# GroupNorm attention over 1024 rows: the low part of v moved from VectorE to GpSimd, with a new order of both engines' work

## The reference

```
def reference(x, W_qkv, b_qkv):
    g = x.reshape(16, 64, 256, 32, 4)                  # 32 groups of 4 channels
    m, s = mean and variance of g over (rows, tokens, the 4 channels)
    n = ((g - m) / sqrt(s + 1e-5)).reshape(x.shape)
    qkv = einsum('bglc,dc->bgld', n, W_qkv) + b_qkv    # d = 384: q, k, v x 2 heads x 64
    score = softmax(einsum('bghlc,bghmc->bghlm', q, k) / sqrt(128))   # inside each row
    out = einsum('bghlm,bghmc->bghlc', score, v)       # back to (16, 64, 256, 128)
    return x + out
```

## Time and profile before

| what | value |
| --- | --- |
| median of 3 runs | 4220.36 us (4219.55 to 4224.01) |
| the profiled execution | 4225.53 us, span 4223.5 us |
| granted TensorE clock | 0.992 of full speed |
| busy: PE, DVE | 3958.7 us (94%), 3759.4 us (89%) |
| busy: ACT, POOL | 3125.2 us (74%), 2134.7 us (51%) |
| HBM | 134.42 MB read, 134.22 MB written |
| mean busy share of the 16 DMA engines | 0.7 to 0.9 in nearly all slices |

### The profile page before, as it was taken

The page is one execution under the profiler, slowest core; times in us unless marked ns, Lnnn a source line. Parts: engine busy times, 40 slices in busy tenths (PEclk is TensorE's granted clock), DMA queues, the critical chain, the costliest instruction groups (busy, mean ns, idle before and its releaser), DMA issues.

```text
span 4223.5 us, 147348 instructions
## 1 busy us (share of the span) xinstructions
PE 3958.7 (94%) x44133; PEld 2923.8 (69%) x44133; DVE 3759.4 (89%) x7138; ACT 3125.2 (74%) x8193; POOL 2134.7 (51%) x3089
## 2 busy tenths in 40 slices
PE   4999999899999999999999899999999999999998
PEld 3767777677776777767777677776767777677776
DVE  6998989889898898988989889898898989989887
ACT  3777777677776777767777677776777777777776
POOL 1555555455554555545555455554555555555554
PEclk9999999999999999999999999999999999999999
DMA  7999898998998989989899998989989998997878
GB/s 197 198 193 201 196 198 196 191 188 199 195 199 181 193 199 198 198 179 200 194 199 198 180 199 197 197 198 181 197 195 201 196 197 193 197 192 166 165 164 167
DMA packets 2438095, 809.81 MB, mean 192 GB/s; under 512 B 2175232, under 2 KB 2437760, under 8 KB 2437760
## 3 DMA queue, kind: packets, MB, share of 16 engines
q1 hardware_dynamic: 2311040, 679.97, 79.7%
q10 hardware_dynamic: 126720, 125.84, 10.7%
HBM read 134.42 MB, written 134.22 MB: 64 GB/s over the span
## 4 chain that ended last, share of the span: by engine, by line
issue 41%; POOL 26%; DVE 15%; POOLq 5%; PE 5%; DVEq 4%; ACT 2%; DMA 1%; SPq 0%; ACTq 0%
POOL p_hi L600 21%; DVE o_norm L455 9%; POOL x_ring L607 4%; POOLq L156 2%; DVEq L460 1%; PE o_bank L315 1%; DVE neg_max L429 1%; POOL y_ring L616 1%; ACT prob L394 1%; PE qk_bank L277 1%; DVE p_lo L436 1%; PE s_bank L299 1%; DVE v_lo L442 1%; POOLq L616 1%; POOLq L607 1%
## 5 line engine op out<-in xcount | busy, mean ns | idle before, releaser
L616 POOL TENSOR_TENSOR y_ring<-image,o_norm 128x256 f32<-128x256 f32 x1024 | 744.5, 727 | 2015.7 <-DVE o_norm L455 2009.9
L394 ACT ACTIVATE prob<-s_bank,neg_max 128x256 f32<-128x256 f32 x4096 | 1604.4, 481 | 189.8 <-issue 177.2
L375 ACT ACTIVATE qk<-qk_bank,b_in 128x256 f32<-128x256 f32 x2048 | 861.0, 472 | 757.2 <-PE qk_bank L277 755.6
L436 DVE SCALAR_TENSOR_TENSOR p_lo<-prob,p_hi 128x1024 f16<-128x1024 f32 x1024 | 1254.3, 1225 | 174.9 <-POOL p_hi L600 144.6
L429 DVE TENSOR_REDUCE neg_max<-s_bank 128x2 f32<-128x512 f32 x2048 | 1309.7, 681 | 35.8 <-PE s_bank L299 35.8
L299 PE MATMUL s_bank<-qk 64*128 64x256 f32 x8192 | 1172.1, 404 | 30.9 <-issue 30.0
L277 PE MATMUL qk_bank<-xc,w_norm 128*128 128x256 f32 x4096 | 1164.2, 407 | 0.0
L600 POOL TENSOR_SCALAR p_hi<-prob 128x1024 f16<-128x1024 f32 x1024 | 1071.4, 1046 | 22.8 <-ACT prob L394 18.1
L277 PEld LDWEIGHTS qk_bank<-xc,w_norm 128*128 128x128 f32 x4096 | 697.1, 190 | 394.9 <-issue 327.0
L299 PEld LDWEIGHTS s_bank<-qk 64*128 64x128 f32 x8192 | 709.4, 187 | 253.2 <-issue 205.3
L315 PE MATMUL o_bank<-v_hi,pt_lo 128*128 128x65 f16 x8192 | 852.9, 193 | 26.6 <-issue 18.0
(11 more groups left out here) (72 smaller groups left out, 2449.4 us busy)
## 6 DMA issues: line engine op xcount, KB each, us to landing
out_dram<-y_ring SPq DMA_DIRECT2D x512, 256.0 KB, 2.5
image<-in_x_dram ACTq DMA_DIRECT2D x240, 512.0 KB, 4.3
pt_hi<-p_hi SPq DMA_TRANSPOSE x1024, 3.3
pt_lo<-p_lo SPq DMA_TRANSPOSE x1024, 3.1
image<-in_x_dram SPq DMA_DIRECT2D x4, 2048.0 KB, 16.2
w_in<-in_L_conv_W_qkv_dram SPq DMA_DIRECT2D x1, 192.0 KB, 2.3
b_in<-in_L_conv_b_qkv_dram SPq DMA_DIRECT2D x3, 0.5 KB, 2.1
```

What stands on the lines that cost most here:

```text
L375: ins = act.activation(qk[:, v % 2, t, :], qk_bank[:, t * TOK:(t + 1) * TOK], ACT.Identity, bias=b_in[:, t:t + 1])
L394: ins = act.activation(prob[:, m, c:c + TOK], s_bank[m][h][:, a * TOK:(a + 1) * TOK], ACT.Exp, bias=neg_max[:, m, h, a:a + 1])
L436: dve.scalar_tensor_tensor(out=p_lo[:, v % 2, :], in0=prob[:, v % 2, :], scalar=P_SCALE, in1=p_hi[:, v % 2, :], op0=ALU.mult, op1=ALU.subt ...
L616: pool.tensor_tensor(y_ring[:, m, :], image[:, par, bass.ds(row, 1), :].rearrange("p a c -> p (a c)"), o_norm[:, v % 2, :, :].rearrange("p ...
```

## The change

The subtraction for `v_lo` goes from DVE to POOL. It no longer reads `v_bank` in PSUM but a new f32 copy `v_full` in SBUF (two buffers), which ACT makes from `v_bank` ahead of `v_hi`; `v_bank` is then free when `v_hi` is done (`project_v` waits for `vhi_done` instead of `vlo_done`), and ACT waits for the `v_lo` of two rows before. POOL's step begins with `p_hi` of row s, then `v_lo` of s, `x_ring` of s+6, `y_ring` of s-4. DVE's step begins with `p_lo` of s-2, then `rsum` and `o_norm` of s-4. The store is one step later. The image loads take two rows each, issued in every second row.

```
--- before.py
+++ after.py
@@ -40,7 +40,8 @@
     LB = ROWS // LOADS
     SETTLE = UNROLL
     LAG = STATS_FROM
-    CHUNKS = ROWS // UNROLL
+    LOAD_ROWS = 2
+    CHUNKS = ROWS // LOAD_ROWS
     QK, PAIR = HEADS * J * TOK, HEADS * J * J
 
     x_img = x.rearrange("n r (p j) c -> n p r (j c)", j=J)
@@ -66,6 +67,7 @@
         p_lo = sb("p_lo", [P, 2, QK], F16)
         pt_hi = sb("pt_hi", [P, 4, PAIR, P], F16)
         pt_lo = sb("pt_lo", [P, 4, PAIR, P], F16)
+        v_full = sb("v_full", [P, 2, J, HEADS, HC])
         v_hi = sb("v_hi", [P, 4, J, HEADS, HC + 1], F16)
         v_lo = sb("v_lo", [P, 4, J, HEADS, HC + 1], F16)
         neg_max = sb("neg_max", [P, 2, HEADS, J])
@@ -176,8 +178,8 @@
                     if what is not None and (place == MEASURE) == (what[0] == MEASURE):
                         share(base, u, par, what, place)
 
-                if coming is not None and u == 0 and bring is not None:
-                    bring(base, *coming)
+                if coming is not None and u % LOAD_ROWS == 0 and bring is not None:
+                    bring(base, u, *coming)
                 order(run, next_image)
 
             def run_image(img, par, first, last):
@@ -188,8 +190,8 @@
                     start = 2 * UNROLL
                     for i in range(-2 * UNROLL, start):
                         if bring is not None and i >= 0:
-                            for c in range(i, CHUNKS - LAG // UNROLL, start):
-                                bring(None, 1, 1, c * UNROLL)
+                            for c in range(i, CHUNKS - LAG // LOAD_ROWS, start):
+                                bring(None, 0, 1, 1, c * LOAD_ROWS)
                         step(i // UNROLL * UNROLL, i // UNROLL * UNROLL, i % UNROLL, par, None, None,
                              (1, 1, ROWS - LAG + i) if i >= 0 else None)
                 else:
@@ -199,12 +201,12 @@
                 with eng.Fori(0, (STATS_FROM - start) // UNROLL) as t:
                     for u in range(UNROLL):
                         step(t * UNROLL + g + start, t * UNROLL + start, u, par, None, None,
-                             None if last else (img + 1, 1 - par, t * UNROLL + (ROWS - LAG + start), first))
+                             None if last else (img + 1, 1 - par, t * UNROLL + (ROWS - LAG + start + u), first))
                 with eng.Fori(0, GROUPS // UNROLL) as t:
                     for u in range(UNROLL):
                         step(t * UNROLL + g + STATS_FROM, t * UNROLL + STATS_FROM, u, par, None,
                              None if last else (MEASURE, img + 1, t * UNROLL + u),
-                             None if final else (img + 2, par, t * UNROLL + (STATS_FROM - LAG)))
+                             None if final else (img + 2, par, t * UNROLL + (STATS_FROM - LAG + u)))
                 for i in range(FINISH):
                     row = ROWS - FINISH + i
                     step(g + row // UNROLL * UNROLL, 0, row % UNROLL, par, row,
@@ -250,7 +252,7 @@
 
             def order(run, next_image):
                 run(-2, transpose_low)
-                run(-6, store)
+                run(-7, store)
                 run(-1, transpose_high)
 
             schedule(sp, order)
@@ -280,7 +282,7 @@
 
             def project_v(base, v, at):
                 if not known_below(base, 1 - v):
-                    pe.wait_ge(vlo_done, base + v)
+                    pe.wait_ge(vhi_done, base + v)
                 pe.matmul(v_bank[:, 0:J * C], half_ones[:, :], vb_split[:, :].unsqueeze(1).broadcast_to([P, J, C]),
                           start=True, stop=False)
                 for j in range(J):
@@ -380,9 +382,11 @@
                 act.wait_ge(v_done, base + (v + 1))
                 if not known_below(base, 4 - v):
                     act.wait_ge(pv_done, base + (v - 3))
-                act.activation(v_hi[:, v % 4, :, :, 0:HC],
-                               v_bank[:, 0:J * C].rearrange("p (j h c) -> p j h c", j=J, h=HEADS),
-                               ACT.Copy).then_inc(vhi_done, 1)
+                bank_view = v_bank[:, 0:J * C].rearrange("p (j h c) -> p j h c", j=J, h=HEADS)
+                if not known_below(base, 2 - v):
+                    act.wait_ge(vlo_done, base + (v - 1))
+                act.activation(v_full[:, v % 2, :, :, :], bank_view, ACT.Copy)
+                act.activation(v_hi[:, v % 4, :, :, 0:HC], bank_view, ACT.Copy).then_inc(vhi_done, 1)
 
             def exponent(h, base, v, at):
                 m = v % 2
@@ -410,10 +414,10 @@
                 run(+1, qk_copy)
                 run(0, v_high)
 
-            def bring(base, img, par, row, free=False):
+            def bring(base, u, img, par, row, free=False):
                 if not (free or base is None or known_below(base, LAG)):
-                    act.wait_ge(y_done, base - (LAG - UNROLL))
-                rows = bass.ds(row, UNROLL)
+                    act.wait_ge(y_done, base + (u + LOAD_ROWS - LAG))
+                rows = bass.ds(row, LOAD_ROWS)
                 act.dma_start(image[:, par, rows, :], x_img[img, :, rows, :]).then_inc(loaded[par], 16)
 
             schedule(act, order, share, bring)
@@ -436,12 +440,6 @@
                 dve.scalar_tensor_tensor(out=p_lo[:, v % 2, :], in0=prob[:, v % 2, :], scalar=P_SCALE,
                                          in1=p_hi[:, v % 2, :], op0=ALU.mult,
                                          op1=ALU.subtract).then_inc(plo_done, 1)
-
-            def v_low(base, v, at):
-                dve.wait_ge(vhi_done, base + (v + 1))
-                dve.tensor_tensor(v_lo[:, v % 4, :, :, 0:HC],
-                                  v_bank[:, 0:J * C].rearrange("p (j h c) -> p j h c", j=J, h=HEADS),
-                                  v_hi[:, v % 4, :, :, 0:HC], ALU.subtract).then_inc(vlo_done, 1)
 
             def sums(base, v, at):
                 dve.wait_ge(pv_done, base + (v + 1))
@@ -575,13 +573,12 @@
                         dve.wait_ge(stat_step, (what[1] + 1) * STAT_STEPS)
 
             def order(run, next_image):
+                run(-2, p_low)
                 run(-4, sums)
                 next_image(0)
-                run(-2, p_low)
                 next_image(1)
+                run(-4, divide)
                 next_image(2)
-                run(-4, divide)
-                run(-1, v_low)
                 run(0, row_max, 0)
                 run(0, row_max, 1)
                 next_image(3)
@@ -599,6 +596,11 @@
                 wait_apart(pool, exp_done, base + (v + 1))
                 pool.tensor_scalar(p_hi[:, v % 2, :], prob[:, v % 2, :], P_SCALE, 1.0, ALU.mult,
                                    ALU.mult).then_inc(phi_done, 1)
+
+            def v_low(base, v, at):
+                pool.wait_ge(vhi_done, base + (v + 1))
+                pool.tensor_tensor(v_lo[:, v % 4, :, :, 0:HC], v_full[:, v % 2, :, :, :], v_hi[:, v % 4, :, :, 0:HC],
+                                   ALU.subtract).then_inc(vlo_done, 1)
 
             def refill(base, v, at):
                 par, row = at
@@ -630,9 +632,10 @@
             pool.wait_ge(first_in[0], 16)
 
             def order(run, next_image):
+                run(0, p_high)
+                run(0, v_low)
+                run(+6, refill)
                 run(-4, finish)
-                run(+5, refill)
-                run(-1, p_high)
 
             schedule(pool, order)
 
```

More of the change, by code:

```diff
@@ L438, in p_low @@
                                          op1=ALU.subtract).then_inc(plo_done, 1)
[L440 to L444, removed]
             def sums(base, v, at):
```

16 lines of the change are left out of this document (9 added, 7 removed).

## The result

The changed kernel takes 4008.05 us (median of 4 runs, 3999.57 to 4012.12) against 4221.4: a ratio of 0.9492, 95% interval 0.9473 to 0.951. The span of the profiled execution is 4010.1 us. The forecast was 4142 us: the direction was right, but the gain, 213 us, is 2.7 times the 79 that were forecast.

The account below looks back on a forecast made before the run. Taken as bound: a POOL and DVE ring, 3.99 us a row, replaced by their shared path at 3.88. Ordinary rows -89, image ends +6, start +5: -78 from 4225.5 is 4147, median 4142; range 3975 to 4300.

Parts of the forecast that it names:

- The ring: POOL and DVE wait in turn through `p_hi`, `p_lo`, `o_norm`, `y_ring`, `x_ring`: 3.99 us a row; cutting it removes 0.67.
- `p_lo` and POOL exclude one another: A DVE operation with two SBUF inputs and a POOL operation block each other, so their times add up.
- The sum of the shared path: `p_hi` 0.99, `v_lo` 0.67, `x_ring` 0.37, `y_ring` 0.73, `p_lo` 1.08, plus 0.04 for change of owner: 3.88 us a row.
- Rival A: POOL and DVE block each other only partly; PE or ACT sets 3.67 to 3.75 us a row: 3956 at 3.72; chance 0.17.
- the next wall if the pace were faster: ACT with the `v_full` copy and load issues needs 3.64 to 3.84 us a row, hidden under 3.88 with little left.
- Loads of two rows cost nothing and bring nothing: Outside the first image, smaller image loads change no bound; a slower landing is free while it stays below two rows.
- The ends of the images, +6 us: Last 12 rows of each image: blocked DVE statistics operations cost 1.7 us, 1.3 gained; +0.4 x 15 = 6.
- Start, +5: First image, first 8 rows: 13 more load issues of 0.85 us each, 11 us, taken as 5.
- Store and refill, 0: Store one row later and refill a row further ahead: no cost; without cover at most 2.5 us once in two rows.
- Rival B: POOL and DVE pay 0.15 us at each of two changes of owner a row: 4343 at 4.08 a row; chance 0.24.

Follow-up runs that it names:

- the exclusion taken away: Changed kernel with `p_lo`'s second input read from PSUM, so it has one SBUF input (its values are others): 3940.89 us, 0.9328.
- late loads of four rows: Changed kernel with ACT's image loads issued behind `xc` and ahead of `qk`, four rows each: 4080.59 us, 0.9664.
- the late place: Changed kernel with ACT's load issued behind `xc` and ahead of `qk` instead of ahead of `prob`: 3961.97 us with two rows a load, 3946.29 with one.
- PE made shorter: Changed kernel without the 8 matmuls of `v_lo` with `pt_hi` in each row: 3955.38 us, 0.936.

## Why the prediction was wrong

- *The ring, and that cutting it moves the bound.* Right. The order alone gave 79 us, and `y_ring` no longer waits.
- *`p_lo` and POOL exclude one another.* Right, and now shown by taking it away: with one SBUF input neither operation grows.
- *The sum of the shared path, 3.84 + 0.04 = 3.88 us.* This step failed; it is 3.66. The term for `y_ring` was its full 0.73; blocked behind `p_lo` it needs 0.58 after the grant, since the first 0.15 us pass in the wait. I had read just this for `p_lo` in the earlier trace rows (1.39 instead of 1.22 + 0.31), and charged the opposite, 0.04, for POOL: -0.19 together. `v_lo` is 0.60 from start to start (0.66 long, not the 0.73 of `y_ring`), not 0.67, and `x_ring` 0.40, not 0.37, because `p_lo` waits for its end: -0.04. `p_hi` is 1.01, not 0.99, and `p_lo` 1.07, not 1.08: +0.01. The sum was also the pace of no more than a part of the rows: 3.66 is PE's own row as well, and PE's with DVE's in the rows with statistics, so where no loads run a path shorter still gains nothing (with the exclusion taken away the last image stays at 3.66). 0.22 us over 1024 rows are 225 us; the total was 134 too high, so some 90 came back: the rows with loads do not reach 3.66, which is the point after next.
- *Rival A.* It held in its place (PE's floor at 3.67, measured 3.65 to 3.66) but for the wrong reason: the exclusion is whole, its sum just equals PE's row. That the two coincide is chance. Its price, 3956, left out the load's stall, worth 46 us, and other rows: the pace with loads is 3.75 to 3.81, not 3.72.
- *ACT "the next wall if the pace were faster".* Right in kind, too coarse as a sum. ACT's copy costs 0.26. ACT is not full (83%); the issue matters because it stands ahead of `prob`, which feeds the full path. Its 0.85 was also too long for the changed kernel: 0.46 more than without a load in the row shown, 0.2 at the median. And an issue is not a fixed part of ACT's row: behind `prob` and `xc` it costs ACT nothing that the trace shows.
- *Loads of two rows cost nothing and bring nothing.* Right for the kernel before (1.0002), wrong for the changed one: 51 us. In the ring there was slack for a late transpose (`p_hi` waited 4.5 us in all for one), on the new path there is none (109.3 us with loads of four rows). The prediction said a slower landing costs nothing below two rows; with late loads of four rows `p_hi` waited for one in 146 rows.
- *The ends of the images, +6 us.* Wrong sign. The small operations are blocked as foreseen (of the 144 two-input operations on `st` over 128x32, 73 take more than 0.4 us, 45 before), but rows 52 to 59 gained 33 us over the 16 images: 20 with the order alone (531.0 to 511.0), the rest with `v_lo` off DVE and smaller loads.
- *Start, +5.* Measured +2.6. *Store and refill, 0.* Nothing in the waits speaks against it (1.9 us for the store).
- *Rival B*, two changes of owner a row at a price: false in sign. Its time for 4.08 was also added up wrongly, with the 5 us between the profiled execution and the median taken off twice: 4225.5 + 80 + 43 + 5 - 5 is 4348, not 4343.
- Open: why the pace of the changed kernel is 3.81 in every other image and 3.77 in the others, and what the rows around the ends of the images needed from PE in the run with PE made shorter.

## What to carry to other kernels

Two engines that share a path must be summed on that path, and each blocked operation counts only from its grant (here 0.15 us less than its length alone); look for the one row where it happened and read both lengths. An engine that is idle may be so while its partner has the path: POOL's 0.96 us here. When two walls stand at the same height, take away each alone and both together; only the last moves the time fully. Issue a DMA behind long work that is already queued on the issuing engine, not ahead of what the critical path waits for. A change that has no effect in a kernel with slack (smaller loads here) is worth trying again once the slack is gone.

## What was not expected of the hardware

- POOL's `y_ring` blocked by a DVE operation with two SBUF inputs ran to 1.70 us and finished 0.58 after it, where it takes 0.73 alone; the DVE operation, started beside `x_ring`, took its turn between two POOL operations that stood back to back.
- 512 KB loads beside the DMA transposes held them up so that `p_hi` waited 252.5 us for them, in 146 rows; with 256 KB it is 52.0 in 42 and with 128 KB 15.1 in 15, all at the late place.
- A load's issue that stands behind `prob` and `xc` in ACT's program ran beside `prob` and left ACT's activations where they were (medians over 459 rows with a load as without); ahead of `prob` it delayed that by 0.2 us at the median.
